# Graph layer kernel: table zeroing in pieces, weight rows broadcast earlier, last block stage divided over four engines

## The chip, the cores and the metric

The kernel runs on one core of a Trainium2 chip. The metric is the device time of one launch in microseconds, median of the runs; three runs of the kernel before are given. The profile is one more execution of the same program, with its own time.

## The reference, cut to what matters

Two graph layers over N = 6250 nodes with 256 features and E = 106,250 edges; `dst` is sorted.

```
msg  = silu(concat(x[src], x[dst], w) @ mW1 + mb1)
msg  = layer_norm(msg) * ln_g + ln_b
msg  = silu(msg @ mW2 + mb2)
agg  = segment_sum(msg, src)
y    = silu(concat(x, agg) @ uW1 + ub1) @ uW2 + ub2
x1   = layernorm(2 * x + y)
sums = segment_sum(x1[src], dst);  mean = sums / max(count, 1)
out  = layernorm(x1 + relu(mean @ W.T + b))
```

All in float32. The kernel keeps P = x @ mW1[0:256] + mb1 and Q = x @ mW1[256:512] as tables: P in memory, to be gathered by `src`; Q on the chip, split in three bf16 parts, to be expanded by `dst`.

## The kernel before, in words

Nodes are cut into 50 blocks (`BLOCKS`) of 125 rows (`NB`); edges into tiles of 128, four tiles (`QT`) to a step, 220 steps. Each engine runs its own program; semaphores order them. The helper `steps` unrolls a loop's first and last rounds and keeps a hardware loop for the middle, `by` rounds in each turn (4 for most loops).

1. *Setup.* The sync queue (SP) loads the edge lists and 15 weight tensors (L323 to L342), then zeroes four sum tables of 6400 x 256 floats in HBM from a tile of zeros, one command a table (L344 to L346), and the pad rows of `p_tab` and `x1_tab`. TensorE (PE) and VectorE (DVE) work out visit tables from the edge lists (L516 to L563, L918 to L1072). VectorE then splits one weight row and one bias into bf16 parts (`split`, L1074 to L1083).
2. *Projection of x* (`pq_step` on SP L353, PE L566, ACT L782, VectorE L1085). A round of SP issues the two loads of x for block q+3, waits for `s_prow`, and issues the two stores of P for block q-1. Each block is cut at row 112, so there are two commands for each (`SPLIT`). PE transposes x and multiplies by 512 columns; VectorE writes P with its bias (`prow`) and the rest parts of Q; ACT the bf16 parts. After the last round SP broadcasts three weight rows into `big` (L369 to L372).
3. *Message stage* (`step_0`), 220 steps. GpSimd gathers rows of `p_tab` and adds the messages into the four sum tables, with indirect DMAs; both wait until the tables and P are complete (L453 to L455).
4. *First block stage* (`block_0`): SP loads four tables a block (L384), VectorE adds them, then the update network, layer norm, and the stores of x1. In it GpSimd copies x rows (L494).
5. *Second aggregation*: GpSimd gathers x1 rows in `ring`, PE sums them by one-hot matmuls (L736), VectorE adds them in `rows` (L1341). `rows` is one tile with all 50 blocks and a count column.
6. *Last block stage* (`block_1`). SP loads x1 of a block into one of two buffers `xin`, waiting for `res` of the block two before (L397 to L400). VectorE scales the sums by 1/count (`mean`, L1359), PE transposes them (L756), ACT copies them out (L900), PE multiplies by W (L765), VectorE adds the bias (L1250), takes relu and adds x1 (L1261), and takes statistics (L1265).
7. *Layer norm and output* (`normalise_all`, L1267). With all statistics VectorE works out 50 means and scales at once, normalises the 50 blocks one by one (L1287), and SP stores them in five groups of ten, in the order 0 to 4, each when its ten are done (`store`, L387).

## Time and profile before

| | us |
|---|---|
| runs: median (lowest, highest) | 4703.93 (4698.99, 4730.17) |
| the profiled execution, its own time | 4717.16 |
| its span, first to last instruction | 4715.4 |
| mean granted clock of PE, of full speed | 0.840 |

Busy over the span: PE 71%, weight loads 52%, VectorE 59%, ACT 34%, GpSimd 66%. In the slices of the page the message stage takes 24 of 40, and the busy shares are averages over stages with different limits; a stage has to be read from its own stretch. The profile names VectorE as DVE, GpSimd as POOL, and the queue of an engine with a q behind it (SPq). A row of the timeline gives the start, the duration, engine, line, operation, tiles, and in brackets the idle time before it and what ended it. A count behind x means that neighbouring instructions are merged, and the duration is then that of all of them. The tiles of the working area all carry the name `arena`.

### The profile page before, as it was taken

How to read it: one execution, taken by the hardware profiler on the slowest of the kernel's cores; microseconds unless marked ns; L12 is line 12 of the kernel's file. 1: busy time of each engine (PE TensorE's matmuls, PEld its weight loads, DVE VectorE, ACT ScalarE, POOL GpSimd, SP SyncE). 2: the span in 40 equal slices, each digit the busy share in tenths (PEclk: the TensorE clock that was granted, in tenths of full speed). 3: DMA queues.
4: the chain of work that ended last, by engine and by line, in shares of the span. 5: the costliest groups of instructions: out<-in, count | busy, mean ns of one | idle time of the engine just before them, and what ended most of it. 6: DMA issues, size and time to landing. Idle time of an engine off the chain costs nothing. (4 is left out here: it accounts for less than half of the span.)

```text
span 4715.4 us, 78508 instructions
## 1 busy us (share of the span) xinstructions
PE 3347.0 (71%) x16589; PEld 2444.8 (52%) x16590; DVE 2799.7 (59%) x13402; ACT 1598.1 (34%) x2993; POOL 3095.4 (66%) x2666
## 2 busy tenths in 40 slices
PE   6777777878887777787778777695555555555564
PEld 3366666666666666666666666574222323223232
DVE  4466666666666666666666666577444444444466
ACT  0355555555555545555555555431000000000001
POOL 0078888888888788878887888612666666666620
PEclk8988899898888988989898888897666676666688
DMA  8345555555555555555555555654333233323213
GB/s 278 100 78 83 83 82 83 83 84 82 83 83 83 82 83 82 83 83 83 82 83 82 83 83 83 123 162 135 88 87 87 85 89 88 89 86 90 86 45 100
DMA packets 311717, 437.83 MB, mean 93 GB/s; under 512 B 49696, under 2 KB 256636, under 8 KB 311420
## 3 DMA queue, kind: packets, MB, share of 16 engines
q0 software_dynamic: 208896, 339.90, 38.6%
q1 hardware_dynamic: 102524, 95.40, 6.8%
q14 instruction: 285, 2.33, 0.2%
q8 instruction: 12, 0.20, 0.0%
HBM read 273.86 MB, written 161.01 MB: 92 GB/s over the span
## 5 line engine op out<-in xcount | busy, mean ns | idle before, releaser
L475 POOL DMA_INDIRECT sum<-arena,sidx x880 | 1403.1, 1594 | 304.2 <-issue 258.8
L463 POOL DMA_INDIRECT arena<-p_tab,idx x880 | 863.2, 981 | 489.7 <-issue 254.4
L736 PE MATMUL ps<-arena 128*125 x1760 | 721.2, 547 | 611.0 <-DVE arena L1341 323.9
L504 POOL DMA_INDIRECT arena<-x_tab,esrc x832 | 796.6, 957 | 500.4 <-PE ps L736 222.3
L648 PE MATMUL ps<-w,arena 128*128 128x256 f32 x3520 | 885.0, 384 | 15.6 <-issue 7.6
L736 PEld LDWEIGHTS ps<-arena 128*125 128x125 f32 x1760 | 391.1, 255 | 941.1 <-issue 892.2
L1341 DVE TENSOR_TENSOR arena<-ps,arena 125x257 f32 x880 | 375.0, 426 | 600.0 <-issue 419.4
L613 PE MATMUL ps<-arena 128*128 128x256 f32 x1760 | 607.2, 506 | 109.1 <-ACT arena L840 106.8
L648 PEld LDWEIGHTS ps<-w,arena 128*128 128x128 f32 x3520 | 601.0, 191 | 149.0 <-issue 25.6
L822 ACT ACTIVATE arena<-ps,key 128x128 f32<-128x128 f32 x880 | 251.5, 369 | 1130.8 <-remote 1081.9
L623 PE MATMUL ps<-ident,arena 128*128 128x128 f32 x1760 | 280.0, 310 | 457.1 <-DVE arena L1173 404.2
L613 PEld LDWEIGHTS ps<-arena 128*128 128x128 f32 x1760 | 434.2, 259 | 222.5 <-issue 145.0
L900 ACT ACTIVATE arena<-ps 128x250 f32<-128x250 f32 x50 | 19.0, 382 | 1418.0 <-PE ps L756 1418.0
L623 PEld LDWEIGHTS ps<-ident,arena 128*128 128x128 f32 x1760 | 218.9, 157 | 493.0 <-DVE arena L1173 347.2
L1150 DVE BATCH_NORM_STATS2 bst<-arena 128x6 f32<-128x256 f32 x880 | 330.7, 418 | 236.4 <-ACT arena L812 204.6
L636 PE MATMUL ps<-arena 128*128 x2640 | 361.6, 291 | 5.7 <-DVE arena L1140 4.9
L1140 DVE TENSOR_TENSOR arena<-ps,arena 128x512 f32<-128x512 f32 x440 | 281.3, 679 | 141.2 <-PE ps L623 59.5
L833 ACT ACTIVATE arena<-ps,gb 128x512 f32<-128x512 f32 x440 | 341.8, 777 | 0.0
L1173 DVE TENSOR_SCALAR arena<-arena,mom,nwt 128x256 f32<-128x256 f32 x880 | 321.0, 426 | 34.8 <-DVE nwt L306 26.5
L636 PEld LDWEIGHTS ps<-arena 128*128 128x128 bf16 x2640 | 279.8, 106 | 100.0 <-issue 29.8
L812 ACT ACTIVATE arena<-arena 128x512 f32<-128x512 f32 x440 | 276.7, 629 | 46.3 <-DVE arena L1140 46.1
L1328 DVE TENSOR_SCALAR arena<-nodes,vloc 128x125 f32<-128x125 bf16 x880 | 202.8, 299 | 121.1 <-issue 66.3
(175 smaller groups left out, 4285.7 us busy)
## 6 DMA issues: line engine op xcount, KB each, us to landing
sum<-zeros SPq DMA_DIRECT2D x4, 6400.0 KB
arena<-sum SPq DMA_DIRECT2D x200, 128.0 KB, 2.1
arena<-p_tab,idx POOLq DMA_INDIRECT x880
sum<-arena,sidx POOLq DMA_INDIRECT x880
arena<-x_tab,esrc POOLq DMA_INDIRECT x832
arena<-x_tab SPq DMA_DIRECT2D x50, 128.0 KB, 2.0
pxin<-in_x_dram SPq DMA_DIRECT2D x50, 112.0 KB
p_tab<-prow SPq DMA_DIRECT2D x50, 112.0 KB
```

What stands on the lines that cost most here:

```text
L463: pool.indirect_dma_start(out=gat[:, par, u, 0:D], out_offset=None, in_=p_tab[:, :], in_offset=bass.IndirectOffsetOnAxis(ap=idx[:, par, u: ...
L475: pool.indirect_dma_start(out=sums[u][:, :], in_=tot[:, par, u, :], in_offset=None, out_offset=bass.IndirectOffsetOnAxis(ap=sidx[:, par, u ...
L504: pool.indirect_dma_start(out=ring[:, tile % RING, 0:D], out_offset=None, in_=x1_tab[:, :], in_offset=bass.IndirectOffsetOnAxis(ap=esrc[:, ...
L613: last = nc.tensor.matmul(ps[:, PM + u // 2, u % 2 * D:(u % 2 + 1) * D], same[:, par, u, :], msg[:, par, u, 0:D], start=True, stop=True)
L623: last = nc.tensor.transpose(ps[:, PZ + h, u * P:(u + 1) * P], act[:, par, u, h * P:(h + 1) * P], ident[:, :])
L636: last = nc.tensor.matmul(ps[:, PP + u // 2, u % 2 * D:(u % 2 + 1) * D], hott[:, par, u, :], big[:, bass.ds(blocks_[u], 1), i, :].rearrang ...
L648: nc.tensor.matmul(to, zt[:, par, h, u * P:(u + 1) * P], w2[:, h, :], start=h == 0, stop=False)
L736: nc.tensor.matmul(ps[0:NB, u, 0:CW], same1[:, par, u, :], ring[:, bass.ds(at[u], 1), :].rearrange("p a c -> p (a c)"), start=True, stop=T ...
L833: nc.scalar.activation(zt[:, par, h, :], ps[:, PZ + h, :], ACT.Identity, bias=gb[:, h, 1:2], scale=gb[:, h, 0:1]).then_inc(s["zev"], 1)
L1150: nc.vector.bn_stats(bst[:, par, u, :], act[:, par, u, :]).then_inc(s["bst"], 1)
L1173: last = nc.vector.tensor_scalar(act[:, par, u, :], act[:, par, u, :], m[:, 4, u:u + 1], nwt[:, par, 3, u:u + 1], ALU.subtract, ALU.mult)
L1341: nc.vector.tensor_tensor(row, ps[0:NB, u, 0:CW], row, ALU.add).then_inc(s["acc"], 1)
```

## The change

- The four zeroing commands of the tables go. In the projection loop SP now issues, in round q, behind the x loads and ahead of the wait for `s_prow`, one zeroing command of 128 rows (128 KB) for each of the four tables: 200 commands. GpSimd waits for their number.
- With that the x loads of blocks 0 to 2 come directly behind the weights and the two pad stores. In round 0 SP waits for the split weight row and issues the broadcast into `big`.
- VectorE's split and bias work moves from behind the visit tables to between the first loop over the counts (L1005 to L1009) and L1011.
- Last block stage: PE transposes `rows` directly, unscaled, and its program is unrolled. ACT, besides the copy of the transposed sums, scales PE's product by 1/count into `hpre`. GpSimd adds the bias into `hpre2`. VectorE has the relu and sum with x1 and the statistics only.
- Normalising: VectorE does groups 0 and 1, ACT groups 2 and 3 (in the form scale * x + shift, the shift being one more small VectorE instruction), GpSimd group 4. SP stores in the order 0, 2, 1, 4, 3.

```diff
+        NORM_ORDER = (("dve", GROUP, 0), ("act", GROUP, 2), ("dve", 2 * GROUP, 1), ("pool", GROUP, 4), ("act", 2 * GROUP, 3))
...
             sp.wait_ge(s_zeroed, 1)
-            for t in sums:
-                sp.dma_start(t.rearrange("(p a) d -> p a d", p=P),
-                             zeros[:, :].unsqueeze(1).to_broadcast([P, SUMROWS // P, D])).then_inc(s_tables, 16)
...
+                if isinstance(q, int) and q == 0:
+                    sp.wait_ge(s_wpart, 5)
+                    sp.dma_start(big[NB:P, :, :, :].rearrange("p j k d -> p j (k d)"),
+                                 w1cp[0:PARTS, :, :].rearrange("p k d -> p (k d)").unsqueeze(1)
+                                 .to_broadcast([PARTS, BLOCKS, PARTS * D])).then_inc(s_wrow, 16)
+                if live(q, BLOCKS):
+                    for t in sums:
+                        sp.dma_start(t[bass.ds(q * P, P), :], zeros[:, :]).then_inc(s_tables, 16)
                 if live(q - 1, BLOCKS):
...
+            for done, count, g in NORM_ORDER:
+                sp.wait_ge(s_norm1[done], count)
+                store(g, out, s_out)
...
-            pool.wait_ge(s_tables, 16 * (TABLES + 2))
+            pool.wait_ge(s_tables, 16 * (TABLES * BLOCKS + 2))
...
+            def add_bias(q, par):
+                pool.wait_ge(s_mean, q + 1)
+                if later(q, 2):
+                    pool.wait_ge(k[1]["res"], q - 1)
+                    pool.sem_inc(s_turn_pool, 1)
+                nc.gpsimd.tensor_tensor(hpre2[0:NB, par, :], hpre[0:NB, par, :], blb[0:NB, :], ALU.add)\
+                    .then_inc(s_biased, 1)
+            steps(pool, BLOCKS, 0, add_bias, by=4)
+
+            pool.wait_ge(s_shift, 1)
+            for q in range(4 * GROUP, 5 * GROUP):
+                nc.gpsimd.tensor_scalar(rows[0:NB, q, 0:D], rows[0:NB, q, 0:D], momb[:, 1, q:q + 1],
+                                        nwb[:, 3, q:q + 1], ALU.subtract, ALU.mult).then_inc(s_norm1["pool"], 1)
...
             def columns_1(q, par):
-                pe.wait_ge(t["agg"], q + 1)
...
-                                               agg[0:NB, par, c * P:(c + 1) * P], ident[0:NB, 0:NB])
+                                               rows[0:NB, q, c * P:(c + 1) * P], ident[0:NB, 0:NB])
...
-                    pe.wait_ge(t["oadd"], q - 1)
+                    pe.wait_ge(s_mean, q - 1)
...
-            steps(pe, BLOCKS, 1, block_1, by=4)
+            pe.wait_ge(e[1]["acc"], QUADS * QT)
+            for q in range(BLOCKS + 1):
+                block_1(q, q % 2)
...
+                if live(q - 1, BLOCKS):
+                    o = 1 - par
+                    ac.wait_ge(t["omm"], q)
+                    if later(q - 1, 2):
+                        ac.wait_ge(s_biased, q - 2)
+                    ac.sem_inc(s_turn_act, 1)
+                    nc.scalar.activation(hpre[0:NB, o, :], ps[0:NB, PM + o, 0:D], ACT.Identity,
+                                         scale=cnt[:, 1, bass.ds(q - 1, 1)]).then_inc(s_mean, 1)
...
+            ac.wait_ge(s_shift, 2)
+            for g in (2, 3):
+                for q in range(g * GROUP, (g + 1) * GROUP):
+                    nc.scalar.activation(rows[0:NB, q, 0:D], rows[0:NB, q, 0:D], ACT.Identity,
+                                         bias=shiftb[:, q:q + 1], scale=nwb[:, 3, q:q + 1]).then_inc(s_norm1["act"], 1)
...
+            def block_1(q, par):
+                result(q, par, 1)
+            steps(dve, BLOCKS, 0, block_1, by=4)
+            block_scales()
+            dve.sem_inc(s_shift, 1)
+            nc.vector.scalar_tensor_tensor(out=shiftb[:, :], in0=momb[:, 1, :], scalar=-1.0, in1=nwb[:, 3, :],
+                                           op0=ALU.mult, op1=ALU.mult).then_inc(s_shift, 1)
+            for q in range(2 * GROUP):
+                normalise(q, s_norm1["dve"])
```

## Rows read from the trace of the kernel before

**Rows 1.** Busy time by stretch: us, instructions; then granted clock, DMA share, GB/s.

```profile
14.00:88.00 74.00, 51.87 (x129) 26.95 (x129) 34.08 (x46) 0.60 (x1) 0.00 (x0) 0.90 1.03 346
97.00:212.00 115.00, 108.76 (x300) 44.60 (x300) 60.16 (x150) 47.99 (x149) 0.00 (x0) 0.99 0.38 106
230.00:3044.00 2814.00, 2221.77 (x13161) 1790.71 (x13162) 1865.89 (x10765) 1462.03 (x2638) 2246.06 (x1744) 0.90 0.52 84
3300.00:4577.00 1277.00, 711.25 (x1736) 384.00 (x1736) 558.59 (x1737) 0.00 (x0) 780.40 (x816) 0.70 0.29 84
4577.00:4680.50 103.50, 67.75 (x300) 44.33 (x300) 74.12 (x202) 19.03 (x50) 0.00 (x0) 0.97 0.22 64
```

**Rows 2.** Timeline from 40 to 98 us: start, us, engine, line.

```profile
40.09 1.07 DVE L1012 TENSOR_TENSOR arena<-arena,ps 128x880 f32<-128x880 f32 x1 [2.27 <-PE ps L546]
...
81.50 1.76 PE L562 MATMUL ps<-ident,arena 128*128 128x128 f32 x7 [4.18 <-DVE arena L1050]
...
90.30 8.08 SPq L359 DMA_DIRECT2D pxin<-in_x_dram  x10
...
92.69 0.28 DVE L911 CAST w1cp<-w1cf 128x256 bf16<-128x256 f32 x1
...
97.26 0.48 DVE L1082 SCALAR_TENSOR_TENSOR b2r<-b2p,ident,b2f 128x256 bf16<-128x256 bf16 x1
```

**Rows 3.** Timeline of PE at the start of the projection.

```profile
102.93 0.38 PE L572 MATMUL ps<-ident,pxin 125*128 125x125 f32 x2
...
104.86 0.38 PE L572 MATMUL ps<-ident,pxin 125*128 125x125 f32 x2
```

**Rows 4.** Timeline of the sync queue in the projection, one loop turn.

```profile
177.97 0.87 SPq L365 DMA_DIRECT2D p_tab<-prow  x2
179.04 0.87 SPq L359 DMA_DIRECT2D pxin<-in_x_dram  x2
...
187.24 0.87 SPq L365 DMA_DIRECT2D p_tab<-prow  x2
```

**Rows 5.** Waits of the sync queue, 96 to 213 us: total, times, longest.

```profile
SPq L365 <- DVE prow L1091: 8.2, 7, 3.3
```

**Rows 6.** Groups by line and form, 4577 to 4716: busy, mean ns, idle before.

```profile
L765 PE MATMUL ps<-wt,arena 128*125 128x256 f32 x200 | 54.1, 395 | 0.2 <-ACT arena L900 0.2
...
L756 PE MATMUL ps<-ident,arena 125*128 125x125 f32 x100 | 22.0, 304 | 35.5 <-DVE arena L1359 35.5
```

**Rows 7.** Busy time by stretch, in the stores of the result.

```profile
4690.00:4692.00 2.00, 0.00 (x0) 0.00 (x0) 2.00 (x8) 0.00 (x0) 0.00 (x0) 0.50 1.00 296
```

**Rows 8.** L384, loads of the tables: a timeline row, and durations min/median/max in ns.

```profile
3099.98 1.76 SPq L384 DMA_DIRECT2D arena<-sum  x4
...
L384 SPq DMA_DIRECT2D arena<-sum x200: 328/381/1206, 3068.0 to 3225.8; - x100
```

**Rows 9.** Timeline between the projection and the message stage.

```profile
203.89 8.21 SPq L365 DMA_DIRECT2D p_tab<-prow  x10
...
219.68 0.96 POOL L463 DMA_INDIRECT arena<-p_tab,idx  x1 [0.30 <-issue]
...
225.16 0.58 PE L593 MATMUL psh<-identh,arena 128*128 128x128 bf16 x4 [14.56 <-DMA arena<-w1cp]
...
229.43 1.29 DVE L1140 TENSOR_TENSOR arena<-ps,arena 128x512 f32<-128x512 f32 x2 [14.15 <-PE ps L636]
```

**Rows 10.** DMA issues by line: count, KB each, median us from issue to landing.

```profile
arena<-x_tab SPq DMA_DIRECT2D x50, 128.0 KB, 2.0
```

**Rows 11.** Timeline of the last block stage.

```profile
4646.49 0.42 DVE L1261 SCALAR_TENSOR_TENSOR arena<-arena 125x256 f32 x1 [0.18 <-DVE arena L1250]
...
4647.13 2.19 SPq L400 DMA_DIRECT2D arena<-x_tab  x2
4647.16 0.43 DVE L1265 BATCH_NORM_STATS2 bstb<-arena  x1 [0.24 <-DVE arena L1261]
```

**Rows 12.** Durations of GpSimd's copy L494, min/median/max in ns.

```profile
L494 POOL COPY arena<-arena x50: 403/605/982, 3065.2 to 3225.9; 125x256 f32 x46, 125x256 f32<-125x256 f32 x4
```

**Rows 13.** The chain that ended last, 4576 to 4585 us.

```profile
4578.99 2.08 PE ps L765 x4
```

More of the change, by code:

```diff
@@ L117, in gnn @@
         cnt = sb("cnt", [NB, 2, BLOCKS])
+        shiftb = sb("shiftb", [NB, BLOCKS])
         work = arena[:, BIG_W:BIG_W + WORK_W]
@@ L385, in _, with store @@
             steps(sp, BLOCKS, 0, load_0)
-            def store(l, to):
-                for g in range(BLOCKS // GROUP):
-                    sp.wait_ge(k[l]["norm"], GROUP * (g + 1))
-                    for a, z in SPLIT:
-                        sp.dma_start(by_place(to, g)[a:z], rows[a:z, g * GROUP:(g + 1) * GROUP, 0:D])\
-                            .then_inc(s_x1st if l == 0 else s_out, 16)
-            store(0, x1_tab[0:N, :])
+            def store(g, to, stored):
+                for a, z in SPLIT:
+                    sp.dma_start(by_place(to, g)[a:z], rows[a:z, g * GROUP:(g + 1) * GROUP, 0:D]).then_inc(stored, 16)
+            for g in range(BLOCKS // GROUP):
+                sp.wait_ge(k[0]["norm"], GROUP * (g + 1))
+                store(g, x1_tab[0:N, :], s_x1st)
             sp.wait_ge(s_x1st, STORES)
@@ L1283, in normalise_all, with normalise @@
                 dve.wait_ge(t["newt"], NEWTON_OPS)
[L1285 to L1291 removed]
+            def normalise(q, done):
+                row = rows[0:NB, bass.ds(q, 1), 0:D].rearrange("p a d -> p (a d)")
+                nc.vector.tensor_scalar(row, row, momb[:, 1, bass.ds(q, 1)], nwb[:, 3, bass.ds(q, 1)],
+                                        ALU.subtract, ALU.mult).then_inc(done, 1)
             t = k[0]
@@ L1312, in _ @@
             steps(dve, BLOCKS, 5, block_0, by=4)
-            normalise_all()
+            block_scales()
+            with dve.Fori(0, BLOCKS // GROUP) as g:
+                for j in range(GROUP):
+                    normalise(g * GROUP + j, t["norm"])
             s = e[1]
@@ L1352, in _ @@
             t = k[1]
-            def mean(q, par):
-                sums_ = rows[0:NB, bass.ds(q, 1), 0:D].rearrange("p a d -> p (a d)")
-                if later(q, 2):
-                    dve.wait_ge(t["cols"], q - 1)
-                nc.vector.tensor_scalar(agg[0:NB, par, :], sums_, cnt[:, 1, bass.ds(q, 1)], None, ALU.mult)\
-                    .then_inc(t["agg"], 1)
-            def block_1(q, par):
-                if live(q, BLOCKS):
-                    mean(q, par)
-                if live(q - 2, BLOCKS):
-                    result(q - 2, par, 1)
             dve.wait_ge(s["acc"], QUADS * QT)
```

68 lines of the change are left out of this document (30 added, 38 removed).

## The prediction

> **What bounds the kernel now.** I read first the busy time by stage, because the change touches only the two ends of the program. [rows 1] cut the span: the projection of x (97 to 212 us), a seam (212 to 230), the message stage (2,814 us), the second aggregation (1,277 us), the last block stage (103.5 us), and the stores of the result. The two long stages, 87% of the span, are not edited; the buffers, loops and queues in them stay, so I leave them at zero. The reader should see in the same rows which engine or queue each edited stage leans on.
>
> From 14 to 88 us the transfers saturate their engines (share 1.03, 346 GB/s): that is the zeroing of the four tables, 25.6 MB in four commands, in the same queue as all else. Behind them stand the first loads of x, issued from 90.30 [rows 2]. But the projection does not start late by much because of that: TensorE's previous work ends only with the transposes at 81.5, and VectorE, which every projected block needs, is busy with the visit tables and the weight splits until 97.7 [rows 2]. PE starts its first x transpose at about 97 and VectorE follows some 4 us later.
>
> The projection runs 50 blocks. TensorE's own pace, where nothing holds it, is 1.93 us a block (L572 at 102.93 and 104.86, [rows 3]). The steady pace is slower, and the next view says why: in [rows 4] the sync queue's own instructions repeat with 9.27 us for four blocks (177.97 to 187.24), 2.32 us a block, its eight pairs of DMA commands nearly back to back, each pair 0.87 long and 1.07 from start to start, plus one loop turn. [rows 5] agree: in 115 us this queue waited 8.2 us for VectorE's blocks, and for nothing else of that size. So the queue's issuing is the bound of this stage, not the DMA engines (share 0.38) and not PE.
>
> The last block stage is set by VectorE: four instructions a block (mean L1359, bias L1250, relu and sum L1261, statistics L1265), 202 instructions and 74 us busy in 103.5, the rest being dependent gaps. PE waits 35.5 us there for L1359 [rows 6]. After that the stores: the DMA share is 1.00 soon after the first of them [rows 7], so they are bound by transfer and not by the normalising.
>
> **The change part by part.**
>
> *Table zeroing moved into the projection loop.* Four big commands go; 200 small ones of 128 KB come (50 blocks by 4), on the queue that bounds the stage. Their price as commands: the trace has four such 128 KB commands in a row in the first update stage, 1.76 us for 4 with one at 0.38 [rows 8], so (1.76 - 0.38) / 3 = 0.46 us from start to start. Bounds: commands with fixed addresses come at 8.21 / 10, about 0.41 (L365 x10, [rows 9]); commands that each work out an own address come at 1.07 / 2 = 0.535 [rows 4]. The four zero pieces share one offset q*128, as the four loads of [rows 8] share theirs, so I take 0.46, and 0.1 a block for that offset (the difference of 0.535 and 0.41, rounded). Loop turn of four blocks: 9.27 + 16 x 0.46 + 0.4 = 17.0, so 4.26 us a block; with 0.41 it is 3.96, with 0.535 it is 4.46. None of it hides: the queue can't work ahead, since at step 1 it waits for the first transpose of x and then for VectorE's first block. Two of the 50 pieces fall before that, 48 after.
>
> The DMA engines are no new bound: a block then moves 512 KB of zeros and 250 KB of x and P, at the 296 GB/s of [rows 7] some 2.5 us, under 4.26. PE needs 1.93 a block and has slack; even at half clock (twice 1.93) it stays under 4.26.
>
> *x ahead in the queue, and the splits moved.* The x loads now stand ahead of all zeroing and land long before 81.5, so PE can transpose and multiply two blocks as soon as its transposes of 81.5 are over. VectorE's split and bias work (92.69 to the L1082 end at 97.74, 5.05 us) moves to where VectorE waits for the counts, ahead of L1012 at 40.09. The gap there is 2.27 long [rows 2], so the work pushes the visit chain by 2.8 us; the PE work at L557 (34 us) follows from it and shifts too. VectorE is free for the projection at 92.7 + 2.8 = 95.5, writes block 0 by 95.9, and the queue has stored it by 96.9.
>
> From there: steps 2 and 3 and 44 to 46 are unrolled, with fixed addresses, 4 x 0.41 + 4 x 0.45 = 3.44 each (17.2); 40 steps in the loop at 4.26 (170.4); steps 47 to 49 without x loads 2.6 each (7.9); the last store 0.8. Sum 196.3, end at 293.2. Before, the last store was issued by 203.89 + 8.21 = 212.1. The queue ends 81.1 us later.
>
> *Weight rows broadcast at the start.* Before, that one command stands behind the last store at 212.14, and PE does nothing until it has landed, 225.16; the first sum with gathered rows (L1140) starts at 229.43 [rows 9]. Now it has long landed. What is late next: GpSimd's gathers, which wait for all P stores and all zero pieces. 293.2 + 2.0 for landing (the 128 KB loads of x1 take 2.0, [rows 10]) + 4 gathers at 0.96 + 0.30 = 5.0 [rows 9] + 2.0 again for the last of them = 302.2. Against 229.4: **+72.8 us**, of which the broadcast has given back some 8. With 0.41 a piece +61, with 0.535 +81.
>
> *Last block stage.* Removed from VectorE: mean and bias. PE transposes the raw rows, ACT evacuates and later scales the product by 1/count, GpSimd adds the bias, VectorE keeps two instructions. Demand per block: PE at most 2 x 0.22 + 4 x 0.27 = 1.5 (L756 and L765, busy over count in [rows 6]); ACT two instructions of 0.38; VectorE two instructions of 0.43 and the 0.24 between them [rows 11], about 1.1; GpSimd one addition, an operation the trace lacks. Its nearest row is the copy L494 of the same shape, 403 to 982 ns, median 605 [rows 12]. Bounds 0.40 (the copy's lowest) and 1.21 (twice its median, as it reads two tensors); I take 0.6, the median of the row it is nearest to. 
>
> None of these is the pace. What is late next is x1: the load of block q waits until VectorE has used block q-2 (two buffers, L399). In [rows 11] L1261 starts at 4646.49 and lasts 0.42, the queue issues the load at 4647.13, 0.22 later, it lands after 2.0, and then comes the next L1261 of that buffer: 0.22 + 2.0 + 0.1 + 0.42 = 2.74 for two blocks, 1.37 a block. Before, at 2.06 a block, that latency was hidden. First L1261: start 4577.0, transposes 0.45, ACT 0.39, product 2.08 (the first one, [rows 13]), ACT 0.38, addition 0.6, hand-overs 0.3: 4581.2. Then 49 x 1.37 = 67.1 and 1.0 for the last statistics: 4649.3 against 4680.5. **-31.2 us.**
>
> *Normalising shared.* VectorE does its first ten rows as before and the first store starts as early (3.3 us in); from there the DMA engines are at about 1.00 [rows 7] with 6.4 MB to move, so more engines bring nothing. One more small instruction, +0.2. I count 0 to -1.
>
> Sum: 72.8 - 31.2 + 0.2 = **+42 us**. Made against the profiled execution (4717.16 us, span 4715.4), that is 4759; the runs' median is 13 us lower, so 4703.9 + 42 = **4746 us**.
>
> **Rivals.**
>
> *A, slower: each zero piece costs as much as an x piece.* If the commands pay for an address each, or their 128 rows slow the x and P pairs, the step is 4.46 us, the front +81, the sum +50, and some more if the pairs grow: 4756. For it: the 128-row commands of [rows 8] last 0.38 at the median, while a whole pair of x or P commands is over in 0.87. It decides (over 1%, 47 us) from 4.38 us a block.
>
> *B, slower: GpSimd's addition and VectorE's L1261 exclude each other.* The copy L494 ranges from 403 to 982 ns while VectorE runs two-input operations beside it. If the addition takes 1.2 and L1261 can't run in it, a block takes 1.2 + 0.43 + 0.2 = 1.8, the last stage gains 10 instead of 31: sum +63, 4767. It decides from an addition of 0.75 us on. Beside it stands a rule of the Trainium skill (SBUF — State Buffer, Who interferes with whom): VectorE's operations with two SBUF inputs and GpSimd's reads hold one port pair by turns; the copy's spread agrees, the size at this place no row shows.
>
> *C, the pieces hide.* If the queue took them at the speed of the transfers, 2.5 us a block, the projection ends near 224, the first L1140 comes at 233, +4: with -31 the time is 4677. Against it: the periodic queue of [rows 4].
>
> *D, everything brings what it frees.* Zeroing free, projection 5.7 earlier, broadcast 8, last stage 31: 4659, just under 1% faster. It needs the queue idle, which [rows 5] deny.
>
> **How the numbers follow.** The forecast case has 0.55 (own range 4732 to 4755, mostly within 1%), A 0.17, B 0.18, C 0.04, D 0.06. A measurement of this kernel can tell about 1% (47 us) from no change. Slower by over 1%: 0.12 of the forecast, 0.14 of A, all of B: 0.44 with the rest of small cases; faster 0.05 from D and a base that was slow; within 1% 0.51. Range 4720 to 4778: below it C and D, above it A and B together (4777).
>
> **What would show it.** In the profile after: the sync queue between about 97 and 293 with groups of eight commands, 17 us for four blocks, and hardly a wait; PE at 0.45 busy there; the first L1140 near 302. The last stage near 72 us, with VectorE waiting for x1's load and not for GpSimd; if GpSimd is named, B. The stores as before, some 27 us from first to last. Wrong would make it a queue step under 3.5 us, or an x1 load that is not waited for.

## The result, and the profile after

| | before | after |
|---|---|---|
| runs: median (lowest, highest), us | 4704.26 (4698.99, 4730.17) | 4758.99 (4750.17, 4765.74) |
| the profiled execution, its own time | 4717.16 | 4764.01 |
| its span | 4715.4 | 4762.1 |

The ratio is 1.011, with a 95% interval from 1.007 to 1.014: slower by about 1%, at the edge between the predicted case "within 1%" and "slower by over 1%". The median of after lies 13 us above the 4746 that was forecast, inside the range of 4720 to 4778, and 4 us above the narrower 4732 to 4755 of the forecast case alone.

The busy time by stretch of the kernel after (start and end of the stretch, its length, busy us and instructions of PE, weight loads, VectorE, ACT and GpSimd, granted clock of PE as a share of full speed, DMA share, GB/s): the projection, the last block stage, and the stores.

```profile
97.00:293.00 196.00, 130.42 (x283) 47.49 (x281) 56.84 (x141) 44.96 (x140) 0.00 (x0) 0.84 0.59 185
4651.00:4726.50 75.50, 63.32 (x298) 47.80 (x296) 44.24 (x104) 37.75 (x100) 36.25 (x50) 0.95 0.29 87
4726.50:4762.00 35.50, 0.00 (x0) 0.00 (x0) 11.66 (x38) 9.94 (x20) 12.72 (x10) 0.50 0.62 180
```

Against [rows 1] the projection has grown from 115 us to about 196, and the last stage has shrunk from 103 us to 75. One turn of the projection loop on the sync queue (SPq), four blocks, from the timeline of after; the count behind x is that of merged commands:

```profile
224.29 0.94 SPq L360 DMA_DIRECT2D pxin<-in_x_dram  x2
225.43 1.84 SPq L369 DMA_DIRECT2D sum<-zeros  x4
227.47 0.86 SPq L374 DMA_DIRECT2D p_tab<-prow  x2
228.60 0.87 SPq L360 DMA_DIRECT2D pxin<-in_x_dram  x2
...
241.59 0.94 SPq L360 DMA_DIRECT2D pxin<-in_x_dram  x2
```

224.29 to 241.59 is 17.30 us for four blocks, 4.32 a block, where [rows 4] show 2.32. The four zeroing commands take 1.84 together; the pairs of x and P are about as long as before. The waits of that queue over the projection (97 to 293 us), the whole list:

```profile
SPq L374 <- DVE prow L1128: 0.4, 1, 0.4
```

[rows 5] had 8.2 us there. The queue is now never short of work, and the others wait for it: VectorE stood 102.2 us ahead of its writes of `prow`, waiting for the stores of P. The seam behind it, from the timeline of after:

```profile
294.16 1.98 SPq L374 DMA_DIRECT2D p_tab<-prow  x4
...
298.83 1.18 POOL L468 DMA_INDIRECT arena<-p_tab,idx  x1 [293.31 <-issue]
...
305.54 1.29 DVE L1177 TENSOR_TENSOR arena<-ps,arena 128x512 f32<-128x512 f32 x2 [7.69 <-DMA arena<-p_tab,idx]
```

The first sum with gathered rows starts at 305.54 and waits for the gathers, no longer for the weight rows; in [rows 9] it started at 229.43. That is **+76.1 us**.

The last stage of after. First its opening, GpSimd's addition (L519) and VectorE's sum with x1 (L1298), other rows left out; the number in brackets is the idle time before, and what ended it:

```profile
4656.08 0.72 POOL L519 TENSOR_TENSOR arena<-arena,blb 125x256 f32<-125x256 f32 x1 [0.94 <-ACT arena L930]
...
4656.83 0.43 DVE L1298 SCALAR_TENSOR_TENSOR arena<-arena 125x256 f32<-125x256 f32 x1 [0.61 <-POOL arena L519]
...
4657.31 0.73 POOL L519 TENSOR_TENSOR arena<-arena,blb 125x256 f32<-125x256 f32 x1 [0.51 <-DVE arena L1298]
...
4658.07 0.43 DVE L1298 SCALAR_TENSOR_TENSOR arena<-arena 125x256 f32<-125x256 f32 x1 [0.23 <-POOL arena L519]
...
4659.37 0.42 DVE L1298 SCALAR_TENSOR_TENSOR arena<-arena 125x256 f32<-125x256 f32 x1 [0.31 <-DMA arena<-x_tab]
```

Then all 50 of L1298 (least, median and most ns; start of the first and the last) and what its engine waited for ahead of it:

```profile
L1298 DVE SCALAR_TENSOR_TENSOR arena<-arena x50: 424/426/974, 4655.2 to 4725.0; 125x256 f32 x44, 125x256 f32<-125x256 f32 x6
...
  DMA arena<-x_tab: 11.8, 26
  POOL arena L519: 7.0, 10
```

49 steps in 69.8 us are 1.425 us a block; before, the sums of [rows 11] took 97.9 us for the same 49 steps, 2.00 a block. In the opening GpSimd's addition and L1298 follow each other at 1.23 us; from the fourth block on VectorE waits for the load of x1 (26 times, 11.8 us), and the chain of waits names that load for 36.2% of the last 122 us, the longest share. One of these loads came late, and a fifth of the wait for loads is this one:

```profile
4711.52 0.42 DVE L1298 SCALAR_TENSOR_TENSOR arena<-arena 125x256 f32 x1 [2.19 <-DMA arena<-x_tab]
```

This step took 3.28 us; the median from one L1298 to the next but one is 2.75 us, 1.37 a block. From VectorE's reciprocal to the start of the last statistics it is 102.9 us before and 74.9 after: **-28.0 us**.

The tail, by line, in the profile of after:

```profile
L525 POOL TENSOR_SCALAR arena<-arena,momb,nwb x10: 1214/1286/1496, 4730.1 to 4741.6; 125x256 f32<-125x256 f32 x10
...
L938 ACT ACTIVATE arena<-arena,shiftb,nwb x20: 583/587/601, 4730.4 to 4739.7; 125x256 f32<-125x256 f32 x20
```

From the start of the last statistics to the end of the span it was 35.3 us (4680.1 to 4715.4) and is 36.5 (4725.6 to 4762.1): **+1.2 us**. The untouched middle, from the first gathered sum to the reciprocal, took 4347.8 before and 4345.2 after, -2.6. The four make 76.1 - 2.6 - 28.0 + 1.2 = 46.7, the difference of the spans. The medians are 54.7 apart: the profiled execution of before lay 13 us above its median, that of after 5.

The middle is not edited in any kernel below either, and in the fourteen profiled executions, these two included, it takes between 4335 and 4374 us. A single span therefore can't be read more finely than some 20 us; the edited stages are read from their own rows, where they agree to about one.

### The profile page after: what moved, and what is told of

It reads as the page before. It is cut to its first block and busy times, and to the rows that moved or that the text cites. A ratio compares the mean times of both kernels' runs of the same rounds, so it can differ in the third digit from the quotient of the medians.

```text
span 4762.1 us, 78890 instructions
## 1 busy us (share of the span) xinstructions
PE 3368.4 (71%) x16589; PEld 2457.0 (52%) x16590; DVE 2749.2 (58%) x13273; ACT 1623.5 (34%) x3063; POOL 3141.3 (66%) x2726
## 3 DMA queue, kind: packets, MB, share of 16 engines
q14 instruction: 285, 2.33, 0.2%
## 5 line engine op out<-in xcount | busy, mean ns | idle before, releaser
L755 PE MATMUL ps<-arena 128*125 x1760 | 707.6, 536 | 632.5 <-DVE arena L1378 317.6
L755 PEld LDWEIGHTS ps<-arena 128*125 128x125 f32 x1760 | 379.1, 249 | 961.0 <-issue 916.6
L642 PE MATMUL ps<-ident,arena 128*128 128x128 f32 x1760 | 292.4, 318 | 406.6 <-DVE arena L1210 304.5
L832 ACT ACTIVATE arena<-arena 128x512 f32<-128x512 f32 x440 | 276.7, 629 | 49.3 <-DVE arena L1177 48.9
```

Of the source, the lines that this page charges most:

```text
L642: last = nc.tensor.transpose(ps[:, PZ + h, u * P:(u + 1) * P], act[:, par, u, h * P:(h + 1) * P], ident[:, :])
L755: nc.tensor.matmul(ps[0:NB, u, 0:CW], same1[:, par, u, :], ring[:, bass.ds(at[u], 1), :].rearrange("p a c -> p (a c)"), start=True, stop=T ...
```

## The experiments

The columns: ratio to before on the same chip with its interval; us a block in the projection, from the 50 starts of `prow` (first to last over 49); us a block in its loop (the median over four steps, divided by four), which leaves the opening out; start of the first gathered sum; us a block in the last stage, first to last over 49.

| kernel | ratio | projection | its loop | first sum | last stage |
|---|---|---|---|---|---|
| before | 1 | 2.24 | 2.32 | 229.4 | 2.00 |
| after | 1.011 (1.007, 1.014) | 4.08 | 4.32 | 305.5 | 1.42 |
| front_only | 1.016 (1.014, 1.018) | 4.08 | 4.32 | 305.2 | 2.01 |
| last_only | 0.994 (0.992, 0.997) | 2.23 | 2.32 | 228.5 | 1.42 |
| one_command | 1.006 (1.004, 1.007) | 3.44 | 3.61 | 273.1 | 1.43 |
| long_rows | 1.003 (1.002, 1.005) | 3.32 | 3.49 | 266.7 | 1.45 |
| tables_early | 0.994 (0.992, 0.996) | 2.45 | 2.33 | 223.6 | 1.46 |
| small_pieces | 1.015 (1.012, 1.018) | 4.16 | 4.14 | 309.5 | 1.40 |
| act_pieces | 0.999 (0.998, 1.000) | 2.94 | 2.95 | 248.5 | 1.47 |
| pool_pieces | 0.993 (0.991, 0.995) | 2.37 | 2.43 | 219.3 | 1.42 |
| one_x_load | 0.999 (0.997, 1.001) | 2.09 | 2.10 | 223.3 | 1.99 |
| x1_four | 0.993 (0.991, 0.995) | 2.41 | 2.33 | 223.5 | 1.24 |
| all_together | 0.988 (0.987, 0.990) | 2.13 | 2.10 | 214.3 | 1.25 |
| pool_together | 0.990 (0.988, 0.991) | 2.24 | 2.21 | 212.9 | 1.25 |

The two columns differ most where the opening holds one long step: 13.2 us in small_pieces, 11.1 in tables_early, 9.4 in x1_four.

### The two halves apart: front_only, last_only

front_only is the kernel before with the new sync queue program of the projection and VectorE's moved splits; last_only is the kernel after with both put back. The core of front_only:

```diff
-            for t in sums:
-                sp.dma_start(t.rearrange("(p a) d -> p a d", p=P),
-                             zeros[:, :].unsqueeze(1).to_broadcast([P, SUMROWS // P, D])).then_inc(s_tables, 16)
...
+                if live(q, BLOCKS):
+                    for t in sums:
+                        sp.dma_start(t[bass.ds(q * P, P), :], zeros[:, :]).then_inc(s_tables, 16)
```

> The kernel before with the front part of the change alone (zero pieces in the loop, broadcast and splits moved); last stage and normalising as before. Theory 1, the sync queue's issuing: a loop turn of four blocks is 17.3 us as in the changed kernel (2.32 to 4.32 us a block), the first L1140 sum comes 76 us later than before, the time is 4704 + 76 = 4780 us, ratio 1.016. Rival, the front's loss is partly given back in the message stage (the changed kernel's stage came out 10.6 us shorter in its profile): 4765 to 4770 us, and the stage is again near 2828 us where before had 2838.5.

> The changed kernel with its front put back as before: only the last block stage and the normalising are divided. Theory 1: the stage ends 27 to 28 us earlier, paced by the x1 load (1.42 us a block), the stores lose 1 us: 4704 - 27 = 4677 us, ratio 0.994. Rival, a gain that needs the front: none or under 10 us, above 4690.

The first gathered sum came at 305.2 and 228.5, the ratios were 1.016 and 0.994. The front costs some 1.6% (74 us of 4726), the last stage gives 0.6% back (27 us), and the two add up: 0.0156 - 0.0057 = 0.0099 against the measured 0.0106. The loss is in the front. The times themselves are some 22 us above the expected 4780 and 4677 because before took 4726 on that chip. The rival of front_only, a part given back in the message stage, did not come: from the first gathered sum to the statistics of the first block it takes 2868 us in front_only, 2859 in before and 2849 in after. With the same front, one is longer and one shorter than before, so this reads as variation between executions.

### What of a zeroing piece costs: one_command, long_rows, small_pieces

The rival reading was that the bytes of the pieces, or their rows, hold the queue back. one_command moves the same 512 KB a block by one command:

```diff
-                if live(q, BLOCKS):
-                    for t in sums:
-                        sp.dma_start(t[bass.ds(q * P, P), :], zeros[:, :]).then_inc(s_tables, 16)
+                if live(q, BLOCKS) and not (isinstance(q, int) and q >= 48):
+                    sp.dma_start(sums[k][bass.ds((q - k) * P, 4 * P), :].rearrange("(p a) d -> p a d", p=P),
+                                 zeros[:, :].unsqueeze(1).to_broadcast([P, 4, D])).then_inc(s_tables, 16)
```

> The changed kernel, but one zeroing command of 512 rows a block in place of four of 128: the same bytes in 52 commands. If the price is one of commands (0.46 us each and 0.1 for the offset), a block takes 2.9 us, the projection is 66 us shorter than in the changed kernel: 4759 - 66 = 4693 us. If the price goes by rows (descriptors), a block still takes 4.2 us: 4755 to 4760. In between, 512 rows cost as much as a share of four: read from the length of the command.

One block of it on the sync queue:

```profile
124.10 0.88 SPq L360 DMA_DIRECT2D pxin<-in_x_dram  x2
125.08 0.55 SPq L368 DMA_DIRECT2D sum<-zeros  x1
125.82 1.48 SPq L378 DMA_DIRECT2D p_tab<-prow  x2
127.50 0.88 SPq L360 DMA_DIRECT2D pxin<-in_x_dram  x2
```

The command itself is cheap, 0.55 us for 512 rows, but the two stores of P behind it grow from 0.87 to 1.48. The pace, 3.61 us a block in a loop turn (116.88 to 131.32), lies between the two theories. From it and the 4.32 of the kernel after I drew a line with two unknowns: 0.24 us for a command and 2.05 ns for a row. The next two kernels were made to break it. long_rows is one_command with the same bytes in rows of 2 KB:

```diff
-        zeros = sb("zeros", [P, D])
+        zeros = sb("zeros", [P, 2 * D])
...
-                    sp.dma_start(sums[k][bass.ds((q - k) * P, 4 * P), :].rearrange("(p a) d -> p a d", p=P),
-                                 zeros[:, :].unsqueeze(1).to_broadcast([P, 4, D])).then_inc(s_tables, 16)
+                    sp.dma_start(sums[k][bass.ds((q - k) * P, 4 * P), :].rearrange("(p b a) d -> p b (a d)", p=P, a=2),
+                                 zeros[:, :].unsqueeze(1).to_broadcast([P, 2, 2 * D])).then_inc(s_tables, 16)
```

> The kernel one_command with the same 512 KB of zeros a block described as 256 rows of 2 KB instead of 512 rows of 1 KB. Theory (what a command costs SyncE goes by its rows): the command costs 0.24 + 256 x 0.00205 = 0.76 us where it cost 1.29 us, the loop takes about 3.1 us a block instead of 3.6, and the time is some 25 us below one_command, ratio to before about 1.000. Rival (the bytes in flight hold the queue back, the DMA engines being 0.72 busy in that stretch): no gain, 3.6 us a block, ratio 1.0055.

small_pieces is tables_early (below), whose loop has no zeroing, with four commands of 16 rows a block added:

```diff
+                if live(q, BLOCKS):
+                    for t in junk:
+                        sp.dma_start(t[bass.ds(q * P, 16), :], zeros[0:16, :]).then_inc(s_junk, 16)
```

> The kernel tables_early, and in the loop of the projection four transfers a block more, each of 16 rows (16 KB) of zeros into tables of its own that nothing reads: the number of SyncE's DMA commands a block is that of the changed kernel, the bytes are an eighth. So it does extra work that nothing needs. Theory (the price of a command on SyncE has a fixed part and a part for each row; the line through the changed kernel's 4.32 us and one_command's 3.61 us a block gives 0.24 us a command and 2.05 ns a row): four small ones cost 4 x (0.24 + 16 x 0.00205) = 1.1 us a block, the loop takes 2.3 + 1.1 = 3.4 us a block, and the time stands some 50 us above tables_early, ratio to before about 1.005. Rival 1 (a command costs the same whatever it moves, 0.46 us or more): 4 x 0.50 = 2.0 us a block, 4.3 us a block, ratio 1.014 as for the changed kernel less its last stage's gain. Rival 2 (only the bytes count): 2.3 to 2.6 us a block, ratio 0.995 to 0.998.

A block of small_pieces on the sync queue:

```profile
173.16 0.87 SPq L369 DMA_DIRECT2D pxin<-in_x_dram  x2
174.22 1.73 SPq L381 DMA_DIRECT2D junk<-zeros  x4
176.14 0.83 SPq L386 DMA_DIRECT2D p_tab<-prow  x2
177.18 0.87 SPq L369 DMA_DIRECT2D pxin<-in_x_dram  x2
```

The line fell on both sides. Four commands with an eighth of the bytes take 1.73 us instead of 1.84, and the loop is nearly as slow as with the full pieces: 4.14 us a block against 4.32, where the line said 3.4 and tables_early, without them, has 2.33. (The first gathered sum, 309.5, is even later than in after, because of the long step in the opening.) Half the rows with the same bytes gained 0.12 us a block (3.61 to 3.49 in the loop), not 0.5. So the price of the pieces in the change is nearly all in their number: 0.43 us a command at 16 rows, 0.46 at 128. The bytes show where one command carries all of them (DMA share 0.73 in one_command's projection): three commands fewer should save 3 x 0.46 = 1.38 us a block and save 0.71 (4.32 to 3.61). The rest is the 0.09 us by which the one command is longer and the 0.6 us by which the two stores behind it are. Why they are, and whether rows or bytes fill whatever is full, these runs leave open.

### Whose time a command is: act_pieces, pool_pieces

```diff
 # act_pieces, in ACT's round of the projection
+                if live(q, BLOCKS):
+                    for t in sums:
+                        nc.scalar.dma_start(t[bass.ds(q * P, P), :], zeros[:, :]).then_inc(s_tables, 16)
                     ac.wait_ge(s_xt, q + 1)
 # pool_pieces, on GpSimd ahead of the gathers
+            with pool.Fori(0, BLOCKS) as it:
+                for t in sums:
+                    nc.gpsimd.dma_start(t[bass.ds(it * P, P), :], zeros[:, :]).then_inc(s_piece, 16)
```

> The changed kernel with the four zeroing commands of a block issued by ACT, at the top of its turn of the projection, instead of by SyncE; the commands and their bytes are the same. Theory (the 0.43 to 0.46 us of a command are time of the queue that issues it): SyncE is back to its 2.24 to 2.45 us a block; ACT has 45 us of work for 47 blocks, 0.96 us each, and 4 x 0.45 = 1.8 us of commands more, 2.8 us, with its waits for TensorE and VectorE up to 3.3 us a block; the first gathered sum comes 40 to 65 us earlier than in the changed kernel (305.5), ratio to before about 0.999 to 1.003. Rival (a command's price is taken in a part that the queues share, so that all eight commands of a block stand in one row whoever issues them): 4.1 us a block, first gathered sum at 305, ratio 1.011 as for the changed kernel.

> The changed kernel with the 200 zeroing commands issued by GpSimd, which does nothing from 40 us until its first gather, back to back in a loop ahead of the gathers. Theory (the price is the issuing queue's): SyncE and the projection go back to 2.24 to 2.45 us a block (last P store near 213); GpSimd's queue takes 0.96 us a command by the pace of the gathers, up to 1.2 by the first of them, so 200 of them last from 40 to 232 or 280 and the first gathered sum comes at 240 to 288, ratio to before 0.997 to 1.007. Rival (a plain transfer costs GpSimd much less than a gather, because no indices are read): done before 213, first gathered sum at 222 to 229, ratio about 0.994. Rival 2 (shared, as above): 4.1 us a block.

From the timeline of act_pieces, the same four commands in ACT's queue (ACTq) and the sync queue's two pairs beside them:

```profile
163.02 0.88 SPq L371 DMA_DIRECT2D p_tab<-prow  x2
163.67 1.89 ACTq L802 DMA_DIRECT2D sum<-zeros  x4
164.20 0.88 SPq L360 DMA_DIRECT2D pxin<-in_x_dram  x2
```

They overlap in time: the pairs stay at 0.88 while ACT's queue spends 1.89 on its four. The price belongs to the queue that issues. The block takes 2.95 us in the loop, near ACT's own 0.96 + 1.8 = 2.8, and the first gathered sum comes 57 us earlier than in the kernel after, with the same commands and bytes. On GpSimd, which has nothing to do at that time, the 200 commands are over long before the last store of P:

```profile
L460 POOL DMA_DIRECT2D sum<-zeros x200: 539/539/962, 39.7 to 171.5; - x100
```

200 in 131.8 us are 0.66 us each, much less than a gather's 0.96 + 0.30, so the second of the three expectations held. They are not quite free for the sync queue. Two of its pairs of x loads, one while GpSimd issues and one when it is done:

```profile
157.14 1.31 SPq L361 DMA_DIRECT2D pxin<-in_x_dram  x2
...
177.21 0.87 SPq L361 DMA_DIRECT2D pxin<-in_x_dram  x2
```

The loop runs at 2.43 us a block, where it was 2.32 before and 2.33 in tables_early. The whole front is then 10 us ahead of the kernel before (219.3), and the ratio falls from 1.011 to 0.993 by this one move.

### The big commands around the first blocks: tables_early

```diff
+            for n in range(XSLOTS):
+                for a, z in SPLIT:
+                    sp.dma_start(pxin[a:z, n, :], x[n * NB + a:n * NB + z, :]).then_inc(s_xload[n], 16)
+            for t in sums[0:2]:
+                clear_table(t)
...
+                if isinstance(q, int) and q == 0:
+                    for t in sums[2:4]:
+                        clear_table(t)
```

> The changed kernel, but four x blocks loaded first and then the tables zeroed by four big commands, none in the loop. Theory 1: VectorE starts the projection at 94 as in the changed kernel, the pace is back at 2.32 us a block, the seam stays short: first sum with gathered rows near 218, 11 us before that of before; with the last stage's 27 that gives 4704 - 38 = 4666 us. Rival, the x loads from block 4 on stand behind the tables' transfers until some 105 us: the projection stops for up to 10 us, 4676.

223.6, behind the 218 of the theory: the rival's stop came, one step of 11.1 us in the opening, and the loop behind it runs at 2.33 as in the theory. The sync queue shows the stop:

```profile
39.12 14.61 SPq L371 DMA_DIRECT2D arena<-w1cp  x1
53.80 27.78 SPq L351 DMA_DIRECT2D sum<-zeros  x2
84.14 16.87 SPq L367 DMA_DIRECT2D pxin<-in_x_dram  x2
101.05 1.95 SPq L381 DMA_DIRECT2D p_tab<-prow  x2
```

Behind big commands a small one is not issued at once: the two loads of one x block take 16.87 us to get out, and the first store of P follows at 101.05 only. So big commands cost nothing in the loop, but they make the queue stand still ahead of it. The 5.8 us gained against before are what the earlier x and weight rows bring less this stop; the two were not measured apart.

### What bounds the projection of before: one_x_load

```diff
-                    for a, z in SPLIT:
-                        sp.dma_start(pxin[a:z, (k - 1) % XSLOTS, :], x[bass.ds(n * NB + a, z - a), :])\
+                        sp.dma_start(pxin[:, (k - 1) % XSLOTS, :], x[bass.ds(n * NB, P), :])\
```

> The kernel before, with each block of x loaded by one transfer of 128 rows instead of one of 112 and one of 13 (the 3 rows beyond the block are loaded and never used). Theory (SyncE's commands set the pace of the projection before too, at 2.32 us a block): 0.24 to 0.35 us a block less, until TensorE's own 1.94 to 2.0 us a block binds, so 10 to 17 us off the time, ratio 0.996 to 0.998. Rival (TensorE's chain for a block was the bound before, SyncE only kept step with it): no change, ratio 1.000.

The pace went from 2.24 to 2.09 us over all blocks and from 2.32 to 2.10 in the loop, the first gathered sum came 6.1 us earlier, and the ratio, 0.999 with 1 inside its interval, can't tell that from nothing. A little less than expected, and another wait took over; the waits of the sync queue there:

```profile
SPq L369 <- DVE prow L1095: 25.2, 40, 3.6
SPq L363 <- PE ps L576: 4.3, 2, 4.0
```

25.2 us of waiting for VectorE's blocks where [rows 5] had 8.2. The queue was the bound of the projection before, but only by 0.22 us a block in the loop; behind it stands the chain through PE and VectorE.

### The last stage: x1_four

```diff
-            def load_1(q, par):
-                if later(q, 2):
-                    sp.wait_ge(k[1]["res"], q - 1)
-                sp.dma_start(xin[:, par, :], x1_tab[bass.ds(q * NB, P), :]).then_inc(k[1][f"load{par}"], 16)
+            def load_1(q, slot):
+                if later(q, XSLOTS):
+                    sp.wait_ge(k[1]["res"], q - XSLOTS + 1)
+                sp.dma_start(pxin[:, slot, :], x1_tab[bass.ds(q * NB, P), :]).then_inc(s_x1load[slot], 16)
```

> The kernel tables_early with four x1 buffers in the last stage instead of two, so that a load is issued three blocks ahead. Theory (the round trip of load, VectorE's sum and the next load, 2.85 us for two blocks, sets the last stage): it leaves the bound, and next comes the alternation of GpSimd's add (0.72 us) and VectorE's sum with x1 (0.5 us), 1.23 us a block as in the first blocks of the stage; 49 x (1.425 - 1.23) = 9.5 us off tables_early, ratio to before about 0.992. Rival 1 (GpSimd's add and VectorE's instruction don't exclude each other, the first blocks only looked so): 0.9 to 1.0 us a block, 22 us off. Rival 2 (the round trip was not the bound): no change from tables_early.

1.243 us a block (4578.0 to 4638.9), as expected, and 10.8 us less than tables_early for the stage. No load is waited for any more:

```profile
L1306 DVE SCALAR_TENSOR_TENSOR arena<-arena,pxin x50: 409/484/712, 4578.0 to 4638.9; 125x256 f32 x44, 125x256 f32<-125x256 f32 x6
...
  POOL arena L527: 7.3, 14
```

So the round trip of the load was the bound of the stage after the change, worth 0.2 us a block. The pace came as expected, but not by the alternation that I expected. From the timeline of x1_four:

```profile
4610.11 0.73 POOL L527 TENSOR_TENSOR arena<-arena,blb 125x256 f32<-125x256 f32 x1 [0.45 <-DVE arena L1306]
...
4610.54 0.58 DVE L1306 SCALAR_TENSOR_TENSOR arena<-arena,pxin 125x256 f32 x1
...
4611.30 0.73 POOL L527 TENSOR_TENSOR arena<-arena,blb 125x256 f32<-125x256 f32 x1 [0.46 <-DVE arena L1306]
```

L1306 starts inside the addition (4610.11 to 4610.84) and ends 0.28 behind it, lasting 0.58 instead of 0.43. The kernel after has one that starts 0.04 behind the start of an addition:

```profile
4660.69 0.73 POOL L519 TENSOR_TENSOR arena<-arena,blb 125x256 f32<-125x256 f32 x1 [0.31 <-ACT arena L930]
...
4660.73 0.97 DVE L1298 SCALAR_TENSOR_TENSOR arena<-arena 125x256 f32 x1 [0.35 <-DMA arena<-x_tab]
```

It too ends 0.28 behind it. In the two kernels together 54 of VectorE's sums start inside an addition, and none ends sooner than 0.27 us behind it: those that start late in it keep their 0.43, the earlier ones are held. This is what the Trainium skill (SBUF — State Buffer, Who interferes with whom) describes, two-input operations of VectorE and GpSimd holding one port pair by turns; the rows agree. The other way round little is seen: an addition that starts inside L1298 (4659.63 in the kernel after) takes 0.75 instead of 0.72.

The price is small. The 50 of L1306 take 25.8 us in all, and would take 21.3 at 0.426: 0.09 us a block. In three of four blocks VectorE has no idle time ahead of L1306, so there it is itself the bound, with 1.08 to 1.18 us from one L1306 to the next; in the fourth it waits 0.34 for the addition. That the next addition waits for VectorE is also due to the two `hpre2` buffers. How much of the 1.24 would be left with more of them was not tried.

### All that gained, in one kernel: all_together, pool_together

all_together is x1_four with x by one 128-row command a block, the fourth table zeroed behind the last store of P, and this for the normalising, with GpSimd's loop taken out:

```diff
-        NORM_ORDER = (("dve", GROUP, 0), ("act", GROUP, 2), ("dve", 2 * GROUP, 1), ("pool", GROUP, 4), ("act", 2 * GROUP, 3))
+        NORM_ORDER = (("dve", GROUP, 0), ("act", GROUP, 2), ("dve", 2 * GROUP, 1), ("dve", 3 * GROUP, 3), ("act", 2 * GROUP, 4))
```

pool_together is all_together with the zeroing of pool_pieces (its loop on GpSimd, above) in place of the four big commands.

> What the runs so far point to, in one kernel: three tables zeroed by one command each around the first blocks of x, the fourth behind the last P store; x by one 128-row command a block (2.09 us a block where before took 2.24); weight rows broadcast ahead; the changed kernel's last stage with four x1 buffers (1.24 us a block); the normalising by VectorE (30 rows) and ACT (20) without GpSimd. Theory: first gathered sum at 215 to 224 instead of 229.4 (6 to 14 us; the fourth table moves 6.5 MB, 22 us at 296 GB/s, and ends in time for the first addition near 230), last stage 103.6 - 65 = 38 us less, tail 0 to 2 us less than the changed kernel's: 45 to 53 us off the time, ratio 0.989 to 0.991. Rival 1 (the fourth table's zeroing is in the way of the first gathers and the first additions wait for it): up to 20 us of it given back, ratio 0.993 to 0.995. Rival 2 (GpSimd's normalising ran beside the stores at no cost): tail as in the changed kernel.

> The kernel all_together, with its four big zeroing commands replaced by the 200 small ones on GpSimd's queue, as in pool_pieces (0.64 us a command there, over by about 170 us, ahead of the last P store). Theory: SyncE keeps the pace of all_together's loop, 2.1 us a block, and since nothing of the zeroing stands in front of the first blocks or behind the last one, the first gathered sum comes at 207 to 214 instead of 214.3: 0 to 7 us less than all_together, ratio to before 0.987 to 0.988. Rival (GpSimd's transfers slow SyncE's commands, as pool_pieces hints with pairs of 1.06 to 1.16 us where 0.87 was usual): 2.3 us a block or more, first gathered sum at 215 to 222, ratio 0.989 to 0.990.

all_together is the fastest: 4672.32 us against 4724.95 on that chip, ratio 0.988 (0.987 to 0.990), about 1.2% faster than the kernel before. The first gathered sum came at 214.3 and the last stage runs at 1.25 a block. In the tail VectorE normalises 30 rows of blocks in the 9.78 us from 4640.19, 0.326 each; in the kernel after, with GpSimd beside it, it had 20 of them at 0.42. From the last statistics to the end it is 35.8 us, against 36.5 after and 35.3 before. Over all kernels that piece is 34.7 to 35.3 with the normalising of before (three kernels), 35.9 to 36.7 with GpSimd's share (nine), and 35.8 and 35.7 in the two without it. So GpSimd's share cost about 0.5 us, and the divided form without it is still about 0.7 longer than the old one. pool_together starts the first gathered sum 1.4 us earlier (212.9), but can't be told from all_together by its ratio (0.990, the intervals overlap); its rival was half right, the projection takes 2.24 us a block instead of 2.13. From the last start of `prow` to the first gathered sum it takes 10.1 us, all_together 15.0: there VectorE waits 10.6 us for the gathers instead of 5.6. That fits the first rival of all_together, the fourth table's zeroing in the way of the first gathers, at a quarter of its price.

## Why the prediction was right or wrong

**The bound of the projection: right.** The prediction named the sync queue's issuing, against DMA engines and PE. The queue's waits went from 8.2 to 0.4 us, the DMA share is 0.59, and small_pieces shows nearly the same pace in the loop (4.14 against 4.32) with an eighth of the bytes. act_pieces and pool_pieces show it from the other side: 2.95 and 2.43 us a block with the same commands in another queue.

**The price of a piece: right, from the right row.** 0.46 us from [rows 8], and 1.84 / 4 = 0.46 measured. The loop turn was put at 17.0 and is 17.30, 4.32 us a block instead of 4.26. Rival A (4.46) did not come, and its point of decision, 4.38, was close.

**The start of the projection: wrong, in the change's favour, and of no use to it.** The splits were to push the visit chain by 2.8 us; they ran partly inside the waits for the counts, from 36.18, and pushed it by 1.07. VectorE wrote the first block at 93.77, not at 95.5. The queue's end did not follow, because in the unrolled rounds and in the loop it was a little slower than assumed: the last store was out at 296.1 instead of 293.2. From there to the first gathered sum it took 9.4 us where 9.0 were counted. In sum +76.1 against +72.8, a miss of 3.3 us: 2.9 at the queue's end and 0.4 behind it. From the first store of P to the last the queue took 201.2 us where 196.3 were counted, so the pace was 4.9 us off and the early start hid 1.9 of it.

**The weight rows: right.** The first gathered sum no longer waits for them, and the wait for the gathers took their place, 7.69 us long.

**The last stage: mechanism and price right, 3 us off by what a median leaves out.** The first L1298 was expected 4.2 us behind the reciprocal and came after 4.5. The load of x1 binds, as the waits and x1_four show. Its round trip was put at 2.74 us for two blocks, and the median is 2.75. The 49 steps still took 69.8 us where 67.1 were counted, -28.0 in place of -31.2, and 1.9 of these 2.7 us are the one late load above, a step of 3.28 instead of 1.37. Such steps of 2.8 to 3.3 us stand in three of the eight profiled kernels with this last stage and two buffers. Why a load comes late no run shows.

**GpSimd's addition: the number wrong, without effect.** 0.6 was taken from the median of [rows 12]; it is 0.724, least 0.721, and varies hardly at all. In the kernel after it cost some 1 us in the whole stage (22.25 us for the 50 of L1298, against 21.3), in x1_four 0.09 us a block. B's 1.8 us a block took the addition for 1.2. The 1.23 us of the opening are no sign of it: by the program those additions need only the L1298 of two blocks before, and they start 0.21 and 0.20 us behind the end of ACT's L930, as the next two do (0.27 and 0.20), for which the profile names ACT.

**The normalising: the sign wrong.** 0 to -1 was counted, with +0.2 for the shift; it is +1.2. The step that failed is "the first store starts as early" with "more engines bring nothing", which left out that they can cost: GpSimd's operation takes 1286 ns a block, and VectorE's own goes from 0.326 to 0.42 us from start to start beside it, so that the first store starts 8.8 us behind the last statistics where it was 8.1. The stores then take 22.2 us to issue instead of 20.9. About 0.5 us of the 1.2 go with GpSimd's share; where the rest comes from was not tried.

**PE's share of the projection: wrong.** It was expected 0.45 busy; it is 130.42 / 196 = 0.67. The 1.93 us a block is the interval in the opening, where nothing holds PE, and not its busy time: [rows 1] give 108.76 / 50 = 2.18 us a block at a granted clock of 0.99. In the kernel after the clock fell to 0.84, as below, and the busy time rose to 130.42 / 50 = 2.6. PE was not the bound in either case.

**Together.** 76.1 - 28.0 + 1.2 = 49.3 in the edited parts against the +42 of the sum, the difference being 3.3 in the front, 3.2 in the last stage and about 1 in the tail, all three against the change. On the profiled executions that is +49.3 - 2.6 = 46.7; the 54.7 between the medians are not explained beyond the variation of the middle. front_only and last_only confirm the parts in the ratio: +1.6% and -0.6%.

## What to carry to other kernels

A stage whose DMA queue has no idle time is priced in commands first (here the bytes showed only where one command carried 512 KB or more): count the commands a round on that queue and multiply by the interval between two of them in the trace (0.43 to 0.46 us here); a transfer that "spreads" well over the DMA engines may still cost its full price in the queue. Before giving such a queue more to do, look which other engine stands idle at that time, since with the same 200 commands on SyncE the first gathered sum comes at 305.5 and with them on GpSimd at 219.3, 86 us earlier, for 0.11 us a block that they cost the loop there. And when work is taken off the engine that bounds a stage, look at once for the round trips that its slowness had hidden: here a load with two buffers; 10.8 us hung on it where the stage had gained 28.

## What the runs showed of the hardware

- A DMA command on the sync queue costs 0.43 us at 16 rows of 1 KB, 0.46 at 128, and 0.55 at 512; on ACT's queue 0.46 to 0.47 at 128 rows, beside the other queue and without slowing it; on GpSimd 0.66, while most of SyncE's pairs of x loads took 1.06 to 1.31 us instead of 0.87. The Trainium skill (DMA: Bandwidth & Descriptors, SWDGE vs HWDGE vs iDMA) sends plain transfers to SyncE or ACT; here the dearer command on the idle engine was the better one.
- Where one command carries 512 KB, it is itself short, and the next two commands last 0.6 us longer. Behind 13 MB in two commands a pair of small ones took 16.87 us, 15.7 of them one command, while the DMA share was 1.05 from 90 to 101 us.
- A VectorE sum of two tensors that starts inside GpSimd's addition of two tensors ends 0.27 us or more behind it: 0.97 us instead of 0.43 when it starts 0.04 us into the addition, 0.58 at 0.43, 0.48 at 0.53, and 0.43 from about 0.6 on.
- PE's granted clock in the projection went with its pace. In the kernel after, at 4.32 us a block in the loop, it was 0.79 to 0.91 in stretches of 36 to 40 us, so PE was at 1.2 GHz for a part of that time, and front_only and small_pieces show 0.77 to 0.87; in one_command, at 3.61 us a block, it was 1.00 from 137 to 257 us, as in long_rows (3.49):

```profile
177.00:217.00 40.00, 26.11 (x54) 9.39 (x54) 11.28 (x28) 8.65 (x28) 0.00 (x0) 0.79 0.57 179
```

```profile
177.00:217.00 40.00, 26.73 (x68) 9.76 (x68) 13.41 (x34) 10.69 (x35) 0.00 (x0) 1.00 0.73 220
```

The first row is of after, the second of one_command: about the same busy time, for 54 matmuls and for 68.
- On GpSimd a subtract and multiply with two scalars a row, 125x256, took 1286 ns, and an addition of two tensors of that size 724. I had expected the reverse, as the addition reads two tensors.
